# A feed-forward pass on Trainium2: two thirds of each group's product on GpSimd, one third on VectorE

## What is computed

```python
def act_qdq(x):
    qmax = 2.0 ** (ACT_BITS - 1) - 1.0            # ACT_BITS = 16
    scale = jnp.maximum(jnp.max(jnp.abs(x)) / qmax, 1e-12)
    return jnp.clip(jnp.round(x / scale), -qmax - 1.0, qmax) * scale
...
x = act_qdq(x)
up = act_qdq(x @ lpbq_dequant(w_up).T)
gate = act_qdq(x @ lpbq_dequant(w_gate).T)
sig = fixed_qdq_u16(jax.nn.sigmoid(gate))
gate = act_qdq(gate * sig)
o = act_qdq(gate * up)
return o @ lpbq_dequant(w_down).T
```

## Time and profile before

| what | value |
|---|---|
| median of 3 runs | 335.3 us (334.34 to 335.79) |
| span of the profiled execution | 339.0 us |
| busy: TensorE, VectorE, ScalarE, GpSimd | 91%, 82%, 76%, 56% |
| fourth pass's products, first start to last maximum | 286.8 to 311.7 us |

### The profile page before, as it was taken

One profiled execution on the slowest core, in us unless ns is written; L12 is line 12 of the kernel. 1 busy time (PEld: TensorE's weight loads), 2 busy tenths in 40 slices (PEclk: granted clock), 3 DMA queues, 4 the chain that ended last, 5 costly groups with the idle time before them and its releaser, 6 DMA issues.

```text
span 339.0 us, 9852 instructions
## 1 busy us (share of the span) xinstructions
PE 307.3 (91%) x3703; PEld 204.9 (60%) x3703; DVE 277.4 (82%) x651; ACT 258.3 (76%) x465; POOL 191.0 (56%) x339
## 2 busy tenths in 40 slices
PE   2899999999899999999999999999976669698996
PEld 1597877778556666666666665854422224247996
DVE  5259989869849999999999994777799995989853
ACT  3268898878858999999998998787797756983940
POOL 3467999883317888868657678300077772663000
PEclk9999999999959999999999999999999989789999
DMA  6881346652201456510000000000000000000134
GB/s 151 252 283 34 94 137 192 198 160 93 66 2 33 143 172 179 168 38 3 5 2 5 4 3 4 1 0 0 2 0 1 0 1 0 0 0 3 31 95 124
DMA packets 23753, 22.69 MB, mean 67 GB/s; under 512 B 3545, under 2 KB 21402, under 8 KB 23578
## 3 DMA queue, kind: packets, MB, share of 16 engines
q1 hardware_dynamic: 22170, 21.78, 20.9%
q10 hardware_dynamic: 1536, 0.28, 0.4%
HBM read 15.75 MB, written 6.31 MB: 65 GB/s over the span
## 4 chain that ended last, share of the span: by engine, by line
PE 59%; DVE 18%; POOL 7%; ACT 7%; issue 6%; DMA 2%; SPq 1%; POOLq 0%; ACTq 0%; DVEq 0%
PE banks L978 9%; PE banks L695 9%; PE banks L751 9%; DVE mxs L1789 8%; PE banks L1037 6%; PE banks L625 4%; DVE nm L1563 3%; PE banks L618 3%; PE banks L773 3%; PE banks L769 2%; POOL rstd L369 2%; ACT ng L1328 2%; PE banks L688 2%; PE banks L764 2%; PE banks L637 2%
## 5 line engine op out<-in xcount | busy, mean ns | idle before, releaser
L1563 DVE TENSOR_REDUCE nm<-banks 128x4 f32<-128x512 f32 x128 | 84.8, 686 | 9.7 <-PE banks L695 6.2
L1236 ACT ACTIVATE PT<-banks,bmask,vmask 128x1024 f32<-128x1024 f32 x64 | 76.8, 1202 | 3.1 <-PE banks L704 0.4
L978 PE MATMUL banks<-X3T,upT 128*128 128x512 f32 x96 | 48.1, 651 | 12.2 <-DVE mxs L1789 8.9
L695 PE MATMUL banks<-kd,qd 32*128 32x128 f16 x512 | 48.0, 219 | 1.3 <-DVE nm L1563 1.0
L565 POOL TENSOR_TENSOR G<-ng,sq 128x1536 int32<-128x1536 int32 (+3 forms) x10 | 27.9, 2792 | 36.4 <-DVE sq L1820 36.4
L1789 DVE TENSOR_REDUCE mxs<-G 128x1 f32<-128x1536 int32 (+3 forms) x30 | 42.2, 1425 | 4.3 <-ACT G L1294 3.8
L978 PEld LDWEIGHTS banks<-X3T,upT 128*128 128x128 f32 x96 | 19.2, 209 | 39.3 <-issue 20.8
L751 PE MATMUL banks<-PT,VP 128*32 128x128 f32 x1024 | 42.1, 283 | 0.0
L695 PEld LDWEIGHTS banks<-kd,qd 32*128 32x128 f16 x512 | 27.2, 93 | 21.5 <-issue 12.3
L1078 ACT ACTIVATE h<-X,shift,rstd 128x128 f32<-128x128 f32 x64 | 26.3, 484 | 10.6 <-POOL shift L414 10.5
L751 PEld LDWEIGHTS banks<-PT,VP 128*32 128x32 f32 x1024 | 24.5, 110 | 10.1 <-issue 3.2
(11 more groups left out here) (198 smaller groups left out, 728.9 us busy)
## 6 DMA issues: line engine op xcount, KB each, us to landing
kd<-k_dram SPq DMA_DIRECT2D x32, 128.0 KB, 2.7
qd<-q_dram SPq DMA_DIRECT2D x32, 128.0 KB, 2.6
ctxg<-in_ctx_dram SPq DMA_DIRECT2D x8, 256.0 KB, 3.2
X3T<-m_dram SPq DMA_DIRECT2D x1, 1792.0 KB, 10.1
out_dram<-y SPq DMA_DIRECT2D x7, 256.0 KB, 2.3
X<-in_x_dram SPq DMA_DIRECT2D x3, 512.0 KB, 9.8
k_dram<-khi SPq DMA_DIRECT2D x7, 128.0 KB, 1.9
k_dram<-klo SPq DMA_DIRECT2D x7, 128.0 KB, 1.9
```

Of the source, the lines that this page charges most:

```text
L695: return pe.matmul(bank(j % 2)[:, s * P:(s + 1) * P], qd[rows(j), n // GB, s, n % GB, :], kd[rows(j), n // GB, s, n % GB, :], start=True, ...
L978: m = pe.matmul(bank(2 + FC * (g % 2) + k), w[:, k * P:k * P + P], grp(X3T, g), start=True, stop=True)
L1236: act.activation(PT[:, a, :], bank(2 + 2 * a, 2), ACT.Exp, bias=bmask[:, n:n + 1], scale=vmask[:, n:n + 1]).then_inc(S["t_exp"], 1)
L1563: V.tensor_reduce(nm[:, n % 2, c:c + NSET], bank(u).rearrange("p (h m) -> p h m", m=P), AX.X, ALU.max, negate=True).then_inc(S["t_max"], 1)
```

## The change

Four things. The split of the product becomes PC = 2 * GT = 1024 for groups 0 to 5, so GpSimd multiplies two thirds of the columns and VectorE one third; group 6 stays at halves (PB = 768), by the new function `product_split`. The split of the first group's `tn` follows PC. Group 7's up levels come in three parts of 512 columns; VectorE multiplies the first and the last third, GpSimd the middle one. Group 7's maximum comes in two instructions, and the order of VectorE's last instructions changes.

```diff
-        PC = FW // 2
-        PL = GT
+        PC = 2 * GT
         PB = FW // 2
...
+        def product_split(g):
+
+            return PC if g < NG - 2 else PB
...
-                nc.gpsimd.tensor_tensor(GI[:, g * FW:g * FW + PC], tn[:, u, 0:PC], un[g % 3][:, 0:PC], ALU.mult
+                w = product_split(g)
+                nc.gpsimd.tensor_tensor(GI[:, g * FW:g * FW + w], tn[:, u, 0:w], un[g % 3][:, 0:w], ALU.mult
                                         ).then_inc(S["c_op"], 1)
             g = NG - 1
             pool.wait_ge(S["c_tn"], NG + 1)
-            pool.wait_ge(S["c_un"], NG)
-            nc.gpsimd.tensor_tensor(GI[:, g * FW:g * FW + PL], tn[:, g % 2, 0:PL], un[g % 3][:, 0:PL], ALU.mult
-                                    ).then_inc(S["c_op"], 1)
+            pool.wait_ge(S["c_un"], NG + 1)
+            nc.gpsimd.tensor_tensor(GI[:, g * FW + GT:g * FW + 2 * GT], tn[:, g % 2, GT:2 * GT], un[g % 3][:, GT:2 * GT],
+                                    ALU.mult).then_inc(S["c_op"], 1)
...
-            for name, value, k in (("c_tn", NG, 6), ("c_tn", NG + 1, 4), ("c_op", NG - 1, 4), ("c_op", NG, 4), ("c_od", NG, 6)):
+            for name, value, k in (("c_tn", NG, 6), ("c_tn", NG + 1, 4), ("c_op", NG - 1, 4), ("c_op", NG, 4), ("c_od", NG + 1, 6)):
...
-            up_levels(NG - 1, slice(0, PL))
-            up_levels(NG - 1, slice(PL, FW))
+            for k in range(FC):
+                up_levels(NG - 1, slice(k * GT, (k + 1) * GT))
...
-                product(g, PC)
+                product(g, slice(product_split(g), FW))
...
             dve.wait_ge(S["c_od"], NG - 1)
-            product_largest(g - 1, g - 1, slice(PC, FW))
+            product_largest(g - 1, g - 1, slice(PB, FW))
+            dve.wait_ge(S["c_tn"], NG + 1)
+            dve.wait_ge(S["c_un"], NG)
+            product(g, slice(0, GT))
             dve.wait_ge(S["c_op"], NG - 1)
-            product_largest(g - 1, g, slice(0, PC))
-            dve.wait_ge(S["c_un"], NG + 1)
-            dve.wait_ge(S["c_tn"], NG + 1)
-            product(g, PL)
+            product_largest(g - 1, g, slice(0, PB))
+            dve.wait_ge(S["c_un"], NG + 2)
+            product(g, slice(2 * GT, FW))
+            dve.wait_ge(S["c_od"], NG)
+            product_largest(g, g + 1, slice(0, GT))
             dve.wait_ge(S["c_op"], NG)
-            dve.wait_ge(S["c_od"], NG)
-            product_largest(g, g + 1, slice(0, FW))
-            dve.wait_ge(S["c_mx"], NG + 1)
+            dve.wait_ge(S["c_od"], NG + 1)
+            product_largest(g, g + 2, slice(GT, FW))
+            dve.wait_ge(S["c_mx"], NG + 2)
```

More of the change, by code:

```diff
@@ L1855, in _, with product @@
             dve.wait_ge(S["g_sc"], 4)
-            def product(g, w):
-                V.tensor_tensor(GI[:, g * FW + w:(g + 1) * FW], tn[:, g % 2, w:FW], un[g % 3][:, w:FW], ALU.mult
+            def product(g, c):
+                V.tensor_tensor(GI[:, g * FW + c.start:g * FW + c.stop], tn[:, g % 2, c], un[g % 3][:, c], ALU.mult
                                 ).then_inc(S["c_od"], 1)
```

## The result

| | median | runs |
|---|---|---|
| before | 335.55 us | 4 (334.34 to 340.52) |
| changed | 341.26 us | 4 (338.97 to 342.18) |

A forecast was written before the change was run, and what follows sets the result against it. Bound: the fourth pass, ended last by TensorE's group 5, ScalarE's levels, then VectorE. Terms 0.9 + 0.7 = +1.6 us took the span from 339.0 to 340.6; less 3.7, 336.9 us, range 335.3 to 338.0.

The forecast's parts named there:

- GpSimd's 1024 columns: GpSimd's product in groups 0 to 5, widened from 768 columns: 2.36 us against 1.81, +0.55 us each.
- Products 1 to 4: VectorE's 512-column products of groups 1 to 4: about 1.48 to 1.50 us, standing still until GpSimd's product has ended.
- Period: Time between GpSimd product starts in the fourth pass: 3.08 us instead of 2.80, 0.28 us longer a group.
- From the first `tn` to tn(7): Fourth pass up to group 7's gate levels, which wait for GpSimd's product 5: +0.9 us.
- From the end of GpSimd's product 5: End of the fourth pass, to the last maximum: 7.95 us instead of 7.27, +0.7 us.
- Part (4): Start of the fourth pass's rounds: GpSimd's product 5 ends at 305.3; of 1.65 us, 0.7 was slack and +0.9 arrives.
- the ring: Fourth pass: ScalarE, VectorE and GpSimd hand work round, each waiting for another; claimed 0.28 us longer a group.
- The first (VectorE wins the lock): Group 7: VectorE's first third goes before GpSimd's last product, which is then hidden: -0.8, 336.1 us; chance 0.08.
- the lock: VectorE's two-input product stands still until GpSimd's SBUF-reading product has ended, then needs its own time less 0.14 us.
- The second: Fourth pass: no standing still, VectorE's 512-column products take 0.70 us; 335.5 us, chance 0.10.
- the third: Fourth pass: no standing still, and TensorE's group 5 gets the full clock; 334.1 us, chance 0.04.
- The fourth, on the clock: TensorE's group 6 still at half clock (338.9), or the clock falls between idle products before the down products (339.5); 339, chance 0.06.

The follow-up runs named there:

- the twelve later ones: Second set of runs of the changed kernel, no edit: median 339.12 us against 337.43 for the kernel before, ratio 1.0054.
- the memsets: Changed kernel with GpSimd's products of groups 0 to 6 replaced by two memsets each, which read nothing; VectorE's 512-column products beside a memset took 0.69 and 0.68 us.
- the split alone: Kernel before with only GpSimd's share of groups 0 to 5 raised to 1024 columns, end unchanged: pass 26.76 us, median 337.48 us, ratio 1.0051.
- a second gap filled: Kernel before with eleven idle products ahead of group 5 and six ahead of the transpose behind group 0: pass 25.25 us, median 336.84, ratio 0.9987.

## Why the prediction was wrong

**The level failed, not the mechanism.** The step that failed is in the sum's last lines: "The runs' median is 335.3 (334.34 to 335.79), 3.7 below the span, which I take to be the same for both kernels". The 3.7 us was not a fixed distance between a span and a time, and the sentence ahead of the prediction that a span is somewhat longer than the times of the runs is wrong. Run by run, the time is longer than the same run's span, mostly by 1.8 us (338.97 with 337.2 for the profiled execution of the changed kernel) and never by less than 1.75. The kernel before came at 335.55 again; it was the changed kernel's runs that did not lie 3.7 us below a span of 340.6. By the 1.8 us the profiled execution before was itself a run of about 340.8 us (339.0 + 1.8); the three runs shown, within 1.5 us of one another, came from the short half of a spread that reaches from 334.0 to 341.6. A sign of this stood in the rows: the clock's 0.50 of the earlier trace rows is in a place where it comes and goes, and the page shows another dip at 95 us. I treated the clock as a rival of the change when it is a property of every run. From the span I should have said 339.0 + 1.6 + 1.8 = 342.4 for such a run, or else a range some 3 us wide on either side for two medians of a few runs. The measured 341.26 is a value that single runs of the changed kernel often have: three of those four runs had a mean clock of 0.975, as four of the twelve later ones did. That such a set of four is chance, and not a second effect of the change, is my reading; the later twelve and the means over all runs (2.1 us apart) agree with it, and do not prove it.

**The terms, one by one.** GpSimd's 1024 columns: 2.35 to 2.36 us, forecast 2.36. VectorE's 512 columns alone: 0.69, forecast 0.70. Products 1 to 4: 1.41, 1.48, 1.49 and 1.48, forecast about 1.48 to 1.50. Period 3.07, forecast 3.08. From the first `tn` to tn(7): 19.59 us instead of 18.70, +0.89, forecast +0.9. From the end of GpSimd's product 5 (301.92) to the end of the last maximum (308.03 + 1.80 = 309.83): 7.91 us, forecast 7.95; before it was 7.27, so +0.64 where I had 0.68, rounded to 0.7. Up to the joining it is 7.94 against 7.31, +0.63. Sum 1.51 against 1.6.

**Slack.** Part (4) said that 0.7 us of the ring's longer period was hidden before. It was hidden by TensorE's half clock, and only where group 5 has it: with the idle products ahead of group 5 the kernel before gains the 0.7 us (25.98 to 25.25), and the changed kernel does not (27.49 to 27.51). So the cost is 1.51 or 2.26 us by the run. I took it from one trace as if it were always 1.5. This term was mis-sized for the runs with the clock up: the slack is 0 there and not 0.7, and this part of the forecast error is real.

**The rivals.** The first (VectorE wins the lock) did not happen: it arrived 0.36 us too late, 305.18 against GpSimd's start at 304.82; made to happen, it gives 0.24 us and not 0.8, since the last third then meets the lock; the step that GpSimd's last product would be hidden was wrong. The second and the third (no standing still) are refuted by the products' 1.48 us and by the memsets; the ground given against the third was a little off, since TensorE's idle time ahead of group 5 did shrink, from 3.30 to 3.23 us, and yet the half clock came. The fourth, on the clock, named the right cause in the wrong place: in the trace of the changed kernel group 6 had the half clock for its first part alone (3.10 us at 0.89 from 295.10, against 2.90 at 0.98 before), at no cost to the pass, and the down products began at full clock. What set the two profiled spans apart lies at 95 us and behind 275 us, where the kernels are the same.

## What to carry to other kernels

Before giving GpSimd a larger share beside VectorE, look for instructions of VectorE with two inputs in SBUF that meet its products: here they stood still until GpSimd had ended, so what counts is how far GpSimd's instruction reaches into VectorE's next one, not how the busy time adds up. Of the three shares tried (640, 768 and 1024 columns of 1536) the best was the one where that overlap was 0.13 us, the opposite direction from this change.

Before adding a difference to a median, find which run the profiled execution was: compare its span and mean clock with those of the runs, and read a small change from a stretch of the trace (here within 0.03 us) and not from medians that wander by 1.5 us.

## What was not expected of the hardware

TensorE's half clock makes the span of one unchanged kernel vary from 332.2 to 338.9 us. The twelve traces show it in a few places, each behind idle time of TensorE, and in each place in some runs and not in others:

- At 92 to 101 us it is the dearest. In the trace before (behind waits of 0.77 and 0.21 us) the stretch from 92 to 102 us has a clock of 0.66; in the second trace of the changed kernel, with the same two waits, it has 1.00. That trace is 0.59 us ahead at these waits (92.14 against 92.73) and 3.37 us ahead behind them (the reciprocal on VectorE at 101.99 against 105.36).
- Behind 275 us, with 2.04 to 2.05 us idle ahead, two groups take 7.01 us instead of 5.32.
- At group 5, with 3.23 us idle ahead in both traces of the changed kernel, it is there in one (5.5 us) and not in the other (2.84). In the kernel before it costs 0.73 us of the pass (25.98 against 25.25 with the idle products), in the changed one nothing.
- Two places cost nothing or next to it: the idle products behind 299 us in the changed kernel (with the split alone the half clock reached the transpose behind the pass, whose wait grew from 0.42 to 0.71 us), and 252 to 257 us in the third pass (0.57 from 252 to 256 us, behind 2.08 us idle, in the second trace of the changed kernel, which is still 3.32 us ahead of the trace before at 269 us).
- Three traces have it at 20 us as well, the first of the changed kernel among them (0.83 from 15 to 25 us, behind 2.00 us idle).

So the mean clock of a run tells how long the clock was halved, not how much time that cost. With idle products ahead of group 5 alone, none of twelve runs had a mean clock under 0.985, and the highest span was 338.2 us; with a second gap filled, again none of twelve, and 336.8 us, against 338.9 us in the kernel before.
